# Two transformer layers on one core: totals right behind the values, biases on GpSimd, one VectorE pass per output tile

## The reference

```python
# layer 0
h = ada_norm(x, cond, ln1)                      # (LN(x) g + b)(1 + scale) + shift
q, k = rotary(h @ wq + bq), rotary(h @ wk + bk); v = h @ wv + bv
x = x + softmax(q k^T / sqrt(32)) v @ wo + bo
h = ada_norm(x, cond, ln2)
x = x + gelu(h @ ff_w1 + ff_b1) @ ff_w2 + ff_b2
# layer 1
sh1, sc1, g1, sh2, sc2, g2 = split(silu(c) @ wc.T + bc)
h = LN(x)(1 + sc1) + sh1
x = x + g1 * (softmax(q k^T / sqrt(32)) v @ wo.T)      # 4 key heads
h = LN(x)(1 + sc2) + sh2
x = x + g2 * (gelu(h @ w1.T + b1) @ w2.T + b2)
```

## Time and profile before

| | us |
|---|---|
| median of 3 runs (4398.61 to 4399.73) | 4398.98 |
| the profiled execution's time | 4396.25 |
| its span | 4394.4 |
| PE busy | 3935.9 (90%) |
| DVE busy | 2700.4 (61%) |
| ACT busy | 1545.5 (35%) |
| POOL busy | 1484.7 (34%) |

### The profile page before, as it was taken

The page is one execution under the profiler, slowest core; times in us unless marked ns, Lnnn a source line. Parts: engine busy times, 40 slices in busy tenths (PEclk is TensorE's granted clock), DMA queues, the critical chain, the costliest instruction groups (busy, mean ns, idle before and its releaser), DMA issues.

```text
span 4394.4 us, 52695 instructions
## 1 busy us (share of the span) xinstructions
PE 3935.9 (90%) x20400; PEld 1473.4 (34%) x20400; DVE 2700.4 (61%) x4376; ACT 1545.5 (35%) x1767; POOL 1484.7 (34%) x807
## 2 busy tenths in 40 slices
PE   6888998898988889888898998988899898989998
PEld 4322443223432235322253223422244223432234
DVE  4776646766457764576655776367654776457743
ACT  1355213543124531244421553135521553125521
POOL 2465112651115531165300561026500563015610
PEclk9899999989999999999999999999999999999999
DMA  5131242202422124222131002301032001310022
GB/s 145 44 110 70 71 109 67 66 20 82 107 64 67 39 69 104 73 66 61 58 116 58 8 27 87 108 25 34 29 96 80 22 27 65 111 44 15 32 70 91
DMA packets 126871, 289.56 MB, mean 66 GB/s; under 512 B 14704, under 2 KB 54660, under 8 KB 125728
## 3 DMA queue, kind: packets, MB, share of 16 engines
q10 hardware_dynamic: 57856, 199.79, 13.6%
q1 hardware_dynamic: 68768, 86.40, 8.6%
HBM read 208.78 MB, written 36.20 MB: 56 GB/s over the span
## 4 chain that ended last, share of the span: by engine, by line
PE 76%; DVE 13%; issue 4%; ACT 3%; POOL 3%; ACTq 1%; DMA 0%; SPq 0%; POOLq 0%; DVEq 0%
PE ps L696 11%; PE ps L697 11%; PE ps L698 11%; PE ps L797 9%; PE ps L880 9%; PE ps L861 8%; PE ps L731 6%; PE ps L895 6%; DVE mcol L1376 5%; ACT probs L1050 3%; PE ps L748 2%; POOL sums L635 2%; DVE dcopy L1393 1%; PE ps L712 1%; DVE ring L1426 1%
## 5 line engine op out<-in xcount | busy, mean ns | idle before, releaser
L635 POOL TENSOR_TENSOR sums<-probs 128x1024 f32<-128x1024 f32 x480 | 1136.8, 2378 | 1958.4 <-ACT probs L1050 1195.4
L1376 DVE TENSOR_REDUCE mcol<-ps 128x1 f32<-128x512 f32 x2048 | 1324.2, 680 | 498.1 <-PE ps L797 484.7
L1050 ACT ACTIVATE probs<-ps 128x1024 f32<-128x1024 f32 x1024 | 1022.0, 1022 | 1042.6 <-PE ps L861 912.9
L797 PE MATMUL ps<-ks,qs 97*128 97x512 f16 x2048 | 759.0, 402 | 183.0 <-DVE mcol L1376 177.0
L861 PE MATMUL ps<-qs,ks 98*128 98x512 f16 x2048 | 643.4, 398 | 120.4 <-ACT probs L1050 103.6
L1205 ACT ACTIVATE sums<-ps,cols 128x512 f32<-128x512 f32 x256 | 175.9, 687 | 1195.1 <-PE ps L698 1195.1
L880 PE MATMUL ps<-probs,v_sb 128*32 128x512 f32 x4096 | 578.0, 639 | 1.0 <-ACT probs L1050 1.0
L797 PEld LDWEIGHTS ps<-ks,qs 97*128 97x128 f16 x2048 | 182.1, 98 | 920.5 <-DVE mcol L1376 802.3
L1478 DVE CAST probs<-sums 128x512 f16<-128x512 f32 x256 | 114.9, 449 | 474.2 <-ACT sums L1205 474.1
L696 PE MATMUL ps<-ring,probs 128*128 128x512 f16 x1024 | 388.2, 379 | 6.0 <-DVE probs L1479 6.0
L696 PE MATMUL ps<-aT,ring 128*128 128x512 f16 x1024 | 389.4, 380 | 0.0
(11 more groups left out here) (100 smaller groups left out, 3128.5 us busy)
## 6 DMA issues: line engine op xcount, KB each, us to landing
ring<-halves ACTq DMA_DIRECT2D x256, 512.0 KB, 3.3
qs<-hl SPq DMA_DIRECT2D x192, 128.0 KB, 4.1
ring<-in_weights ACTq DMA_DIRECT2D x39, 512.0 KB, 4.4
halves<-ring ACTq DMA_DIRECT2D x37, 512.0 KB, 2.9
ks<-hl SPq DMA_DIRECT2D x120, 128.0 KB, 4.3
probs<-in_x SPq DMA_DIRECT2D x8, 1024.0 KB, 7.4
ks<-in_x ACTq DMA_DIRECT2D x8, 1024.0 KB, 6.7
x_mid<-ks SPq DMA_DIRECT2D x32, 256.0 KB, 2.7
```

Source lines behind the costliest of these rows:

```text
L635: pool.tensor_tensor(sums[:, m % SUM_SLOTS, :, :], prob(u - 2), prob(u), ALU.add).then_inc(sum_set[0].sem, 1)
L797: pe.matmul(bank, qs[0:K_MAX, qc, h, P * qt:P * qt + P], ks[0:K_MAX, key_set(i, hh), key_head(i, hh, h), 512 * half:512 * half + 512], sta ...
L1050: act.activation(prob(u), ps[:, 2 * p:2 * p + 2, :], ACT.Exp).then_inc(exp_done.sem, 1)
L1376: dve.tensor_reduce(mcol[:, blk % 2, at_:at_ + 1], src, AX.X, ALU.max).then_inc(n_free, 1)
```

## The change

- **Order on PE.** The totals come directly behind the values; all narrow items that stood between or behind them follow.
- **Biases on POOL.** Layer 0's output bias is added to x by POOL in attention, at the places `BIAS_AT`, and the MLP's last bias (times the gate in layer 1) in the forward part by `add_last_bias`: 8 more additions of 128x512 each.
- **One DVE pass.** `residual` in layer 0 and `output` in layer 0 scale the PSUM tile and add it to x in one instruction. In layer 1 `output` only reads PSUM times gate into `turn`, and `output_sum` adds it to x later: four tiles in rounds 16 to 19, the last four at u = 2, 4, 6 and 8 of the next item's attention, whose stores SP issues at s = 6.
- **Moves.** ACT instead of DVE drains layer 0's second-half value tiles (`by_scalar`, with a semaphore of its own), SP instead of ACT issues the first six weight DMAs (at s = 57), and ln2's first half is normalised at u = 117 and transposed in steps 60 and 61.
- **Waits.** POOL waits for all four DMAs of `s_rows` before its first instruction on data.

```diff
+BIAS_AT = (40, 41, 42, 43, 48, 49, 54, 55)
-    if s in (STEPS - 3, STEPS - 2):
+    if s in (STEPS - 4, STEPS - 3):
@@ tensor, attention
-                    for key in keys[one + 1:one + 3]:
-                        narrow(key)
                     m = sum_of(max(u - LAG_D, 0))
                     if u >= LAG_D and u - LAG_D == sum_unit(m):
                         totals(i, m)
-                    for key in keys[one + 3:]:
+                    for key in keys[one + 1:]:
                         narrow(key)
@@ gpsimd
+            def add_bias(i, tt):
+                if tt % 4 == 0:
+                    pool.wait_ge(x_again[tt // 4], 16 * (i + 1))
+                x = x1(i)[:, tt, :]
+                pool.tensor_tensor(x, x, row_bc[:, 0, :], ALU.add).then_inc(xb_set.sem, 1)
+            def add_last_bias(i, th):
+                pool.wait_ge(ln_n, NORMS["ln2", i, th] + 1)
+                if gated(i) and th == 0:
+                    pool.wait_ge(gate_in, 16 * (2 * (i - B) + 3))
+                    pool.tensor_tensor(gate_b2, row_bc[:, 1, :], row_bc[:, 2, :], ALU.mult).then_inc(gb_set.sem, 1)
+                    pool.wait_ge(gb_set.sem, gb_set.at(i, 1))
+                for tt in range(4 * th, 4 * th + 4):
+                    x = x1(i)[:, tt, :]
+                    pool.tensor_tensor(x, x, gate_b2 if gated(i) else row_bc[:, 1, :], ALU.add).then_inc(xy_set.sem, 1)
+                    if layer(i) == 0 and m in BIAS_AT:
+                        add_bias(i, BIAS_AT.index(m))
             pool.wait_ge(s_const, 1)
+            pool.wait_ge(s_rows, 64)
                 deviation("ln2", i, 1)
+                add_last_bias(i, 0)
+                add_last_bias(i, 1)
@@ vector, output
-                    dve.scalar_tensor_tensor(out=ytmp[:, t, :], in0=ps[:, t, :], scalar=1 / WS, in1=row_bc[:, 1, :],
-                                             op0=ALU.mult, op1=ALU.add).then_inc(y_read.sem, 1)
-                for t in range(4):
-                    tt = 4 * th + t
-                    dve.wait_ge(y_read.sem, y_read.at(i, tt + 1))
                     if gated(i):
-                        link(dve.tensor_tensor(ytmp[:, t, :], ytmp[:, t, :], row_bc[:, 2, :], ALU.mult))
-                    dve.tensor_tensor(x1(i)[:, tt, :], x1(i)[:, tt, :], ytmp[:, t, :], ALU.add).then_inc(y_set.sem, 1)
+                        dve.scalar_tensor_tensor(out=turn[:, t, :], in0=ps[:, t, :], scalar=1 / WS, in1=row_bc[:, 2, :],
+                                                 op0=ALU.mult, op1=ALU.mult).then_inc(y_read.sem, 1)
+                    else:
+                        x = x1(i)[:, 4 * th + t, :]
+                        dve.scalar_tensor_tensor(out=x, in0=ps[:, t, :], scalar=1 / WS, in1=x,
+                                                 op0=ALU.mult, op1=ALU.add).then_inc(y_read.sem, 1)
+            def output_sum(i, tt):
+                dve.wait_ge(y_read.sem, y_read.at(i, tt + 1))
+                dve.tensor_tensor(x1(i)[:, tt, :], x1(i)[:, tt, :], turn[:, tt % 4, :], ALU.add).then_inc(y_set.sem, 1)
@@ vector, attention
+                    if gated(i - 1) and u in (2, 4, 6, 8):
+                        output_sum(i - 1, 3 + u // 2)
-                    if u % 2 == 0 and s == WO_AT + 5:
-                        norm_apply("ln2", i, 0)
+                        if s == WO_AT + 3:
+                            norm_apply("ln2", i, 0)
@@ scalar to sync
-                    if u == 117:
-                        first_weights(i)
+                    if s == 57:
+                        first_weights(i)
```

More of the change, by code:

```diff
@@ L225, in wide_before @@
 def wide_before(i, s):
-    return min([WIDE[key] for step, rows in WIDE_AT[i].items() if step >= s for key, a, b in rows if a == 0]
-               + [max(WIDE[key] for rows in WIDE_AT[i].values() for key, a, b in rows) + 1])
+    n = min([WIDE[key] for step, rows in WIDE_AT[i].items() if step >= s for key, a, b in rows if a == 0]
+            + [max(WIDE[key] for rows in WIDE_AT[i].values() for key, a, b in rows) + 1])
+    return [key for key, at in WIDE.items() if n - 2 <= at < n]
 class Count:
@@ L445, in scales_known, with stream @@
             return 3 if layer(i) == 1 else 1 if (kind, i) == ("ln1", 0) else 2
+        def stream(i, n):
+            j = 2 * FC * i + n
+            ch = (8 if layer(i) == 0 else L0_CHUNKS + 5) + n % FC
+            return ring[:, j % RING, :], halves[ch, :, :], w_in[j % RING]
         def prob(u):
@@ L450, in gated, with outputs @@
         def gated(i):
-            return layer(i) == 1
+            return i >= B
+        def outputs(i, n):
+            return (y_set.sem, y_set.at(i, n)) if gated(i) else (y_read.sem, y_read.at(i, n))
         block = ctx.enter_context(nc.Block())
@@ L531, in attention, with first_weights @@
                         put_rows(i, s // 8 + 1)
+                    if s == 57:
+                        first_weights(i)
+            def first_weights(i):
+                if i == 0:
+                    for q in range(15, 18):
+                        sp.wait_ge(sp_out[q % 3], 16 * store_count(0, q))
+                if 1 <= i <= 3:
+                    sp.wait_ge(*freed(("mod", 2 * i - 1)))
+                    if i >= 2:
+                        sp.wait_ge(g_st, 16 * (i - 1))
+                for n in range(RING):
+                    dst, src, done = stream(i, n)
+                    sp.dma_start(dst, src).then_inc(done, 16)
             def forward(i):
@@ L1165, in attention @@
                         stack_high(("q", i, 1, u // 50, (u // 2 + 1) % 2 if u < 50 else (u // 2 - 1) % 2))
+                    if u % 2 == 1:
+                        for key, a, b in WIDE_AT[i].get(u // 2, ()):
+                            if b == 12 and by_scalar(key):
+                                values_out(key)
                     for q, (st, ch) in enumerate(here):
@@ L1511, in forward @@
                         output(i, 0)
+                    if gated(i) and FC <= n < FC + 4:
+                        output_sum(i, n - FC)
+                if gated(i) and j == NB:
+                    for tt in range(4, NT):
+                        output_sum(i, tt)
             dve.memset(eps4[:, 0:4], EPS)
```

103 lines of the change are left out of this document (57 added, 46 removed).

## The result

| | before | after |
|---|---|---|
| median, us | 4399.3 (4 runs, 4398.61 to 4399.73) | 4456.08 (4 runs, 4453.66 to 4460.02) |
| ratio, 95% interval | | 1.0130 [1.0116, 1.0144] |
| span of the profiled execution, us | 4394.4 | 4451.8 |
| mean granted clock | 0.958 | 0.949 |

The changed kernel is 57 us slower. The forecast was 4438 (39 us slower), its range 4360 to 4480.

A forecast was written before the change was run, and what follows sets the result against it. It took PE as the bound in the forward part and waits in attention; terms 54 - 26 + 30 + 32 + 7 - 35 - 23 = +39 gave 4435 us profiled, 4438 for the median, range 4360 to 4480.

The forecast's parts named there:

- forecast A: Whole kernel: order and port cost more than boundaries and tail give, 4438 us, own range 4410 to 4465; chance 0.50.
- term 4: Forward rounds 4 to 8: last-bias additions on POOL hold DVE passes, 4 us an item, +32 us.
- term 7: End of attention: weight DMAs off ACT and earlier ln2 transposes shorten PE's waits, -23 us.
- term 6: Between items: fewer DVE passes ahead of the first trial product shorten PE's wait, -35 us.
- B: Attention: loop behind totals decides, third product's wait falls inside an exponential's; faster, 4364 us; chance 0.29.
- Terms 1 to 3: Attention: the new order of totals and products, +54 - 26 + 30 = +58 us.
- Term 1: Attention steps with totals and five products: third product waits for DVE, 0.64 us at 84 places, +54 us.
- Term 2: Attention steps with three or four products: earlier totals shorten the loop through POOL's add, -26 us.
- Term 3: Step 6 of a block: mfin meets POOL's add and delays the rows item's transposition 1.7 us, +30 us.
- 5, start: Kernel start: POOL's wait for all bias-row DMAs delays the first deviation 15 us, +7 us at the end.
- rival D: Attention and forward part: fast-mode and two-operand DVE passes alternate with POOL's additions everywhere, 4476 us; chance 0.12.

The follow-up runs named there:

- a1: Changed kernel with the totals again behind up to two trial products, as before the change: 4411.57 us.
- b1: Kernel before with only the new order, totals right behind the values at every step: 4436.07 us, ratio 1.0081.
- b3: Kernel before with totals ahead only in steps where two or more products stand behind the values, without step 6 of each block: 4443.63 us.
- b4: Kernel before with totals ahead only in steps where one product stands behind the values, without step 6 of each block: 4394.65 us.
- b2: Kernel before with totals ahead only in step 6 of each block, before the rows item: 4457.47 us, ratio 1.0134.
- a2: Changed kernel with the last biases' additions moved behind forward rounds 9 and 11: 4418.27 us.
- a3: Changed kernel with GpSimd's wait for the bias rows behind its first two deviations and first builds: 4449.76 us.

## Why the prediction was right, and where it was off

The direction and the range held: forecast A, 39 us of loss, where 57 were measured. The 18 us between them are term 4 (10 too low) and term 7 (13 too low), less 4 and 1 by which the order and term 6 were too dear. Against B stands what the steady steps show, the third product's wait in full. By my own terms, in us:

| term | forecast | measured |
|---|---|---|
| 1 to 3, the order | +58 | +54 (trace, steps 2 to 55), 43 of it gone in a1; b1 +39; a1 44.5 |
| 1, third product | +54 | b3 +45 |
| 2, totals sooner | -26 | b4 -4 |
| 3, rows item | +30 | b2 +59 |
| 4, last biases | +32 | 42 by the forward parts of a2, 38 by its time |
| 5, start | +7 | +6.7 in the trace, 6.3 by a3 |
| 6, between items | -35 | -28.1, and -7.6 in the forward parts without term 4: -35.7 |
| 7, end of attention | -23 | +5.5 - 15.1 = -9.6 |

**Terms 1 to 3** have about the right sum out of wrong parts, and that is luck. By layer the sum does not hold: I had +22 for layer 0 and +36 for layer 1; in b1's attentions, with the order alone, it is -13.5 and +54.5, and from a1 to the changed kernel (steps 2 to 55) +8 and +35. Layer 1 carries the cost, and in layer 0 not even the sign is steady. Term 1: +0.50 a place, not 0.64, and 0.31 of it comes back at the next step in four of the twelve places; in layer 0, for which I had 23 us, b3's attentions grow by 3. Even so b3 lost 45, since in layer 1 each item loses 9 to 10 us, of which steps 24 and 48 are 4.2, the first of them shown at the lower clock above. Term 2 failed: I took the loop through POOL's add as the last to end at some ten places an item, and b4 shows that it hardly is; layer 0's -5.8 us in its third block, which I had given to it before these runs, belongs to the rows item (b2 -4.1 there) and the long steps (b3 -1.9). Term 3: the mechanism of step 6 was right to 0.2 us, but it strikes at steps 6, 22, 30, 38 and 46 of a layer 1 item, of which I had priced three, and at step 54 it costs 3.6 us where I had 1.7; in layer 0 the wide items that were to cover it at step 6 did not (+1.6 to +1.9), but steps 23 and 24 gave more than that back. At step 54 the matmuls of the output tile run at half clock behind the wait:

```profile
3157.64 1.28 DVE L1444 TENSOR_TENSOR mfin<-mcol 128x16 f32<-128x16 f32 x1
3159.06 0.27 PE L888 MATMUL ps<-ident,mfin 128*16 128x128 f32 x1 [2.13 <-DVE mfin L1444]
...
3161.55 0.63 PE L760 MATMUL ps<-wo,aT 128*128 128x512 f16 x1
```

0.63 us a matmul instead of 0.38. No term had a price for the clock inside attention; I had one only between the items.

**Term 4** was sized at 4 of at most 6.3 us an item; a2 gives 5.5 to 6.5 for seven items, so up to 0.2 above my bound (the last has no next norm: 0.7). It is rival D's value, and D's mechanism, the fast-mode pass that alternates with the additions, was right for this place. D's other half, 20 us more from mfin, would also have been nearer to b2.

**Term 7** missed by 13 us, the most outside the order. The weights off ACT did what I said. For ln2 I subtracted the add that nm meets and the rest of step 60, and overlooked what is queued on DVE behind them: L1430 waits for totals there, and the second pair of transposes stands behind it.

## What to carry to other kernels

Before two instructions change places, look at what the engine that is to be cheered on waits for next: here a trial product between values and totals was cover for DVE, and taking the cover away cost more than sooner totals gave. Work given to GpSimd costs by where its passes fall, not by their number: the same eight additions cost 38 us beside a norm, where PE waits for DVE, and nothing that shows behind rounds 9 and 11, where DVE has time to spare. A sum that comes out right is no proof of its parts: it took b2, b3 and b4 to see that the order's three terms, each made alone, were 45, -4 and 59 and not 54, -26 and 30. A change of several parts is worth taking apart even when its sum is a loss: three edits made 4456 into 4358, and moving ln2 back made it 4325.

## What the runs showed of the hardware that I had not expected

Four `tensor_scalar` passes with one operand in SBUF took 5.79 us in place of 1.92 beside GpSimd's additions, and a cast 1.49 in place of 0.43. The additions were slowed less: 5.49 for four, against 4.93 for the four behind round 11 in item 5 of a2.

After a wait of 1.72 us in b2 and of 1.78 us in b3 the matmuls ran at 1.2 GHz, while PE was busy in most of the microseconds ahead of it, and after the same wait elsewhere they did not. The fall costs 2.3 us in b2's step 7 (6.06 for 3.79), more than the 1.55 us of the step with the wait. The same step 24 took 5.75 us in the kernel before, with PE's wait of 1.78 us ahead of it and the clock at 1.00, 5.76 in b2 and 7.84 in b3, 0.50 of that by the order itself. b3's step 48 took 6.30 us for 4.16 at a granted clock of 0.73, and there no wait in the ten microseconds ahead of it was longer than 0.96 us.
